# A graph network on one core: two of 208 groups of gathered rows are fetched row by row from two other queues

## The reference

```python
def reference(x, src, dst, edge_weight, edge_weight_n2, ...):       # x: 6250 x 256 f32, 106250 edges, dst sorted
    edge_index = jnp.stack([src, dst])
    x = _layernorm(x + _L0_gnn_ref(x, src, dst, edge_weight, edge_weight_n2, ...))
    x = _layernorm(x + _L1_gnn_ref(x, edge_weight, weight, bias, edge_index, 2))
    return x

def _L1_gnn_ref(feature, edge_weight, weight, bias, edge_index, mode):     # mode 2
    feature = feature - jnp.mean(feature, axis=0, keepdims=True)
    feature = feature / (jnp.std(feature, axis=0, ddof=1) + 0.0001)
    # _spmm: row edge_index[0] of the result is the sum over its edges of edge_weight * feature[edge_index[1]]
    support = _spmm(edge_index, edge_weight, feature, feature.shape[0])
    return support @ weight + bias
```

## Time and profile before

| | |
|---|---|
| median of 3 runs | 3402.89 us (3399.97 to 3411.76) |
| the profiled execution: its own time | 3413.44 us |
| the profiled execution: span of the profile | 3411.7 us |
| busy share of PE, PEld, DVE, ACT, POOL | 73%, 54%, 67%, 31%, 74% |
| DMA packets | 275056, 565.29 MB, mean 166 GB/s |

### The profile page before, as it was taken

One profiled execution on the slowest core, in us unless ns is written; L12 is line 12 of the kernel. 1 busy time (PEld: TensorE's weight loads), 2 busy tenths in 40 slices (PEclk: granted clock), 3 DMA queues, 4 the chain that ended last, 5 costly groups with the idle time before them and its releaser, 6 DMA issues.

```text
span 3411.7 us, 47557 instructions
## 1 busy us (share of the span) xinstructions
PE 2507.6 (73%) x10659; PEld 1840.3 (54%) x10701; DVE 2299.3 (67%) x5450; ACT 1059.9 (31%) x3135; POOL 2529.2 (74%) x2706
## 2 busy tenths in 40 slices
PE   5776766666676666579999999996776665556777
PEld 4555544444344443368888888543444444444565
DVE  7989977777777677657776777786455455555455
ACT  3344333333333333245555555562000000000022
POOL 6777677777777777777777777576777777777775
PEclk8878988888988889799999999998988888887899
DMA  6554344444444444388988999454333333333344
GB/s 163 157 147 126 120 158 154 158 162 155 157 155 156 163 155 156 129 262 285 289 288 284 291 290 292 153 172 136 105 105 105 105 105 105 105 105 106 109 137 120
DMA packets 275056, 565.29 MB, mean 166 GB/s; under 512 B 55599, under 2 KB 121126, under 8 KB 274787
## 3 DMA queue, kind: packets, MB, share of 16 engines
q0 software_dynamic: 119808, 329.02, 30.8%
q1 hardware_dynamic: 146452, 223.99, 20.8%
q10 hardware_dynamic: 8528, 9.30, 0.9%
HBM read 419.19 MB, written 142.88 MB: 165 GB/s over the span
## 4 chain that ended last, share of the span: by engine, by line
POOL 49%; PE 22%; issue 18%; DVE 7%; DMA 2%; ACT 1%; DVEq 1%; SPq 0%; POOLq 0%; ACTq 0%
POOL arena L630 23%; POOL messages L560 21%; PE ps L1152 11%; PE ps L962 8%; POOL arena L554 5%; PE ps L1185 2%; PE ps L1085 1%; DMA messages<-arena 1%; DVE ps L2037 1%; DVE ps L2036 1%; DMA arena<-messages 1%; ACT arena L739 0%; DVE bn L2018 0%; DVE ps L1605 0%; DVE ps L1606 0%
## 5 line engine op out<-in xcount | busy, mean ns | idle before, releaser
L560 POOL DMA_INDIRECT messages<-arena x832 | 803.8, 966 | 264.1 <-issue 249.0
L554 POOL DMA_INDIRECT arena<-in_x,arena x832 | 792.1, 952 | 272.3 <-issue 250.7
L630 POOL DMA_INDIRECT arena<-x_table,wh x832 | 790.0, 950 | 263.2 <-issue 253.4
L1222 PE MATMUL ps<-arena 128*128 x2048 | 603.0, 450 | 367.0 <-SPq L505 366.7
L1222 PEld LDWEIGHTS ps<-arena 128*128 128x128 f32 x2048 | 439.4, 223 | 536.6 <-issue 469.8
L962 PE MATMUL ps<-arena 128*128 128x128 f32 x3328 | 457.8, 296 | 127.6 <-ACT arena L676 89.9
L739 ACT ACTIVATE arena<-ps,arena 128x256 f32<-128x256 f32 x832 | 326.5, 475 | 703.3 <-PE ps L1085 466.0
L962 PEld LDWEIGHTS ps<-arena 128*128 128x128 f32 x3328 | 436.8, 209 | 193.1 <-ACT arena L676 128.9
L1085 PE MATMUL ps<-arena 128*128 128x256 f32 x1664 | 470.7, 434 | 49.6 <-DVE arena L1789 42.2
L2212 DVE TENSOR_TENSOR node_a<-node_a,ps 128x256 f32 x256 | 107.7, 421 | 503.7 <-PE ps L1222 501.6
L1085 PEld LDWEIGHTS ps<-arena 128*128 128x128 f32 x1664 | 364.2, 221 | 78.9 <-issue 23.9
(11 more groups left out here) (287 smaller groups left out, 2981.9 us busy)
## 6 DMA issues: line engine op xcount, KB each, us to landing
arena<-messages SPq DMA_DIRECT2D x464, 260.0 KB
arena<-in_x SPq DMA_DIRECT2D x304, 128.0 KB, 2.8
gate_rows<-arena SPq DMA_DIRECT2D x49, 384.0 KB, 2.4
arena<-gate_rows SPq DMA_DIRECT2D x49, 384.0 KB, 3.0
arena<-in_x,arena POOLq DMA_INDIRECT x832
messages<-arena POOLq DMA_INDIRECT x832, 2.5
arena<-x_table,wh POOLq DMA_INDIRECT x832, 2.8
arena<-in_x SPq DMA_DIRECT2D x48, 256.0 KB, 2.9
```

What stands on the lines that cost most here:

```text
L554: nc.gpsimd.indirect_dma_start(out=big[:, s, j, 0:D], out_offset=None, in_=x, in_offset=bass.IndirectOffsetOnAxis(ap=ids[:, j:j + 1], axis ...
L560: nc.gpsimd.indirect_dma_start(out=messages, out_offset=bass.IndirectOffsetOnAxis(ap=ids[:, j:j + 1], axis=0), in_=big[:, s, j, :], in_off ...
L630: nc.gpsimd.indirect_dma_start(out=last_rows[:, (g + 1) % LAST_ROWS, j * D:(j + 1) * D], out_offset=None, in_=x1_table, in_offset=bass.Ind ...
L1222: last = nc.tensor.matmul(ps[g % LAST_SUMS][:, 0:D], last_hot[h][:, j, :], last_rows[:, bass.ds(k, 1), j * D:(j + 1) * D].rearrange("p o d ...
```

## The change

Groups 170 and 180 (`LATE`) are no longer gathered by GpSimd. Their 2 x 512 rows are fetched one row to a DMA, each from the row number of a register: group 170 by ScalarE's queue, in one piece after the square root of line 852 and before the first finished tile; group 180 by SyncE's, four rows in each of the turns 12 to 139 of its loop over the groups. The two groups have buffers of their own, the ninth and tenth. To have the row numbers on one partition, SyncE stores the two groups' columns of `back_id` to memory in the gates stage and loads them back as one row of 1024 numbers. `slot_row` now holds the buffer in its upper bits, with eight more small operations on VectorE. TensorE takes count and buffer out of it, and shifts before it waits. The semaphores `xs_loaded` are named `rows_loaded` and used for both.

```diff
+LATE = (170, 180)
+ROWS_BITS = 8
...
+        BUFFERS = LAST_ROWS + len(LATE)
+        last_rows = arena[:, BACK_W:BACK_W + BUFFERS * CPG * D].rearrange("p (k c) -> p k c", k=BUFFERS)
...
+        def late_rows(engine, i, first, last):
+            for r in range(first, last):
+                p, j = r // CPG, r % CPG
+                v = engine.value_load(late_row[0:1, i * GE + r:i * GE + r + 1]).with_bounds(min_val=0, max_val=NT * P - 1)
+                engine.dma_start(last_rows[p:p + 1, LAST_ROWS + i, j * D:(j + 1) * D],
+                                 x1_table[bass.ds(v, 1), :]).then_inc(S[f"rows_loaded{i}"], 16)
...
             for t in range(3 * SPAN):
                 gates_load(t, t % GATES)
+            sp.wait_ge(S["back_kept"], 2 * PAIRS)
+            sp.wait_ge(S["back_mm"], 2 * PAIRS)
+            for i, g in enumerate(LATE):
+                sp.dma_start(late_table[i, :, :], back_id[:, g * CPG:(g + 1) * CPG]).then_inc(S["row_kept"], 16)
...
             gates_load(FULL, 0)
+            sp.wait_ge(S["row_kept"], 16 + 16 * len(LATE))
+            sp.dma_start(late_row, late_table.rearrange("(o i) p j -> o (i p j)", o=1)).then_inc(S["row_back"], 16)
...
+            sp.wait_ge(S["row_back"], 32)
+            sp.wait_ge(S["x1_stored"], 16 * (SPANS + 1))
             for g in range(GATHERED):
-                sp.wait_ge(S[f"second_rows{g % LAST_ROWS}"], (g // LAST_ROWS + 1) * 16 * CPG)
+                if g in LATE:
+                    sp.wait_ge(S[f"rows_loaded{LATE.index(g)}"], 16 * (2 * XPAIRS // RING + GE))
+                else:
+                    sp.wait_ge(S[f"second_rows{g % LAST_ROWS}"], rounds_of(g) * 16 * CPG)
                 sp.sem_inc(S["second_landed"], 1)
...
+                if 12 <= g < 12 + -(-GE // 4):
+                    late_rows(nc.sync, 1, (g - 12) * 4, min((g - 12 + 1) * 4, GE))
...
             for g in range(GATHERED):
                 k = g % LAST_ROWS
+                if g in LATE:
+                    continue
                 if g >= LAST_ROWS:
                     pool.wait_ge(S["second_freed"], g - LAST_ROWS + 1)
...
+            act.wait_ge(S["row_back"], 32)
+            act.wait_ge(S["x1_stored"], 16 * (SPANS + 1))
+            late_rows(nc.scalar, 0, 0, GE)
             ready = 0
             for g in range(FIRST_END, LAST + 1):
...
-                    rows = nc.tensor.value_load(slot_row[0:1, g:g + 1], min_val=1, max_val=GATHERED)
-                    k = (rows & (LAST_ROWS - 1)).with_bounds(min_val=0, max_val=LAST_ROWS - 1)
+                    slots = nc.tensor.value_load(slot_row[0:1, g:g + 1], min_val=1, max_val=GATHERED + (BUFFERS - 1 << ROWS_BITS))
+                    rows = (slots & ((1 << ROWS_BITS) - 1)).with_bounds(min_val=1, max_val=GATHERED)
+                    k = (slots >> ROWS_BITS).with_bounds(min_val=0, max_val=BUFFERS - 1)
...
+            link(V.tensor_scalar(buffer_i.bitcast(I32), slot_row, LAST_ROWS - 1, ROWS_BITS, ALU.bitwise_and, ALU.logical_shift_left))
+            link(V.tensor_copy(buffer_n, buffer_i.bitcast(I32)))
+            for i, g in enumerate(LATE):
+                moved = LAST_ROWS + i - (g + 1) % LAST_ROWS << ROWS_BITS
+                link(V.tensor_scalar(buffer_i, parts_n, float(g + 1), float(moved), ALU.is_equal, ALU.mult))
+                link(V.tensor_tensor(buffer_n, buffer_n, buffer_i, ALU.add))
+            link(V.tensor_tensor(parts_n, parts_n, buffer_n, ALU.add))
+            link(V.tensor_copy(slot_row, parts_n))
```

More of the change, by code:

```diff
@@ L107, in gnn_program @@
         weight_row = dram("weight_row", [NT * P])
+        late_table = dram("late_table", [len(LATE), P, CPG], I32)
         node_a = sb("node_a", [P, NTP, D])
@@ L234, in gnn_program @@
         last_hot = [hot[:, k, :, :] for k in range(2)] + [area(hot_at + 2304 + k * GE, [CPG, P]) for k in range(LAST_HOTS - 2)]
-        last_rows = arena[:, BACK_W:BACK_W + LAST_ROWS * CPG * D].rearrange("p (k c) -> p k c", k=LAST_ROWS)
-        assert LAST_ROWS & LAST_ROWS - 1 == 0 and BACK_W <= 4 * D + NC and BACK_W + LAST_ROWS * CPG * D <= COLUMNS_W + 2048
+        BUFFERS = LAST_ROWS + len(LATE)
+        last_rows = arena[:, BACK_W:BACK_W + BUFFERS * CPG * D].rearrange("p (k c) -> p k c", k=BUFFERS)
+        assert LAST_ROWS & LAST_ROWS - 1 == 0 and BACK_W <= 4 * D + NC and BACK_W + BUFFERS * CPG * D <= COLUMNS_W + hot_at
         assert PARTS % (4 * RING) == 0 and PARTS <= NG
+        late_row = area(hot_at + 3840, [len(LATE) * GE], I32)[0:1, :]
         slot_row = low_tab[0:1, 0:PARTS]
+        buffer_i, buffer_n = (area(hot_at + 4928 + k * PARTS, [PARTS])[0:1, :] for k in range(2, 4))
         parts_i, parts_n = (area(hot_at + 4928 + k * PARTS, [PARTS])[0:1, :] for k in range(2))
@@ L330, in units_of, with rounds_of @@
                     (v >> UNIT_BITS).with_bounds(min_val=0, max_val=NU - NT)]
+        def rounds_of(g):
+            return sum(1 for k in range(g % LAST_ROWS, g + 1, LAST_ROWS) if k not in LATE)
+        def late_rows(engine, i, first, last):
[4 more added lines that the diff above has]
+                                 x1_table[bass.ds(v, 1), :]).then_inc(S[f"rows_loaded{i}"], 16)
         def scales_of(g):
@@ L377, in x_load @@
                 sp.dma_start(xs[:, s, :].rearrange("p (t d) -> p t d", t=2),
-                             x[2 * q * P:(2 * q + 2) * P, :].rearrange("(t p) d -> p t d", p=P)).then_inc(S[f"xs_loaded{s}"], 16)
+                             x[2 * q * P:(2 * q + 2) * P, :].rearrange("(t p) d -> p t d", p=P)).then_inc(S[f"rows_loaded{s}"], 16)
             sp.dma_start(xt[0:TAIL, :], x[FULL * P:N, :]).then_inc(S["xt_loaded"], 16)
@@ L972, in x_sum @@
             def x_sum(i, s):
-                pe.wait_ge(S[f"xs_loaded{s}"], 16 * i)
+                pe.wait_ge(S[f"rows_loaded{s}"], 16 * i)
                 nc.tensor.matmul(ps[0][:, :], ones[:, :], xs[:, s, :], start=isinstance(i, int) and i == 1 and s == 0, stop=False).then_inc(S["x_used"], 1)
@@ L1479, in run @@
                 def run():
-                    dve.wait_ge(S[f"xs_loaded{s}"], 16 * (i - X_SHIFT + XPAIRS // RING + 1))
+                    dve.wait_ge(S[f"rows_loaded{s}"], 16 * (i - X_SHIFT + XPAIRS // RING + 1))
                     mean = ps[0][:, 0:D].rearrange("p (o d) -> p o d", o=1).broadcast_to([P, 2, D])
```

## The result

| | before | with the change |
|---|---|---|
| median | 3401.56 us (3399.97 to 3411.76, 4 runs) | 3439.99 us (3436.74 to 3441.84, 4 runs) |
| profiled execution: own time, span | 3413.44 us, 3411.7 us | 3436.74 us, 3434.6 us |

The ratio is 1.0106, with a 95% interval of 1.0093 to 1.0118: slower by 32 to 40 us. Forecast were 3392.8 us, in a range of 3388 to 3405, and a chance of 0.11 for slower.

What follows compares the result with a forecast made beforehand. GpSimd's 832 gathers, 1.254 us each, were taken to bound the last product. Eight fewer save 10.0 us, plus 0.05 us from a TensorE register operation: 3402.9 - 10.1 = 3392.8 us, range 3388 to 3405.

Steps and rivals of the forecast that it cites:

- What one takes: ScalarE's price of a fetched row: load 0.279, arithmetic 0.070, DMA 0.378, gaps 0.17 us, about 0.90 us.
- ScalarE's 512 rows: Group 170's fetch after line 852: 518 us available, 1.01 us a row; 461 us needed, landed 57 us early, no cost.
- Bounds of a row's price: Row fetches on both queues: from 0.63 us up to 1.07 us on SyncE and 0.97 on ScalarE, all said to fit.
- Rival A: The two queues delay each other's row DMAs, group 170 lands 43 us late, GpSimd waits 24 us: 3417 us, chance 0.09.
- Rival B: Register loads take 0.6 us, ScalarE's row 1.22 us, GpSimd waits 88 us: 3481 us, chance 0.02.
- SyncE's turn: SyncE's loop over groups: a turn with four rows takes 3.8 us and fits in a group's 5.02 us.
- the price of a gather: GpSimd in the last product: 1.254 us each, so eight gathers fewer save 10.0 us.
- TensorE caught up: TensorE in the last product: group 171's work comes 5.02 us early, absorbed after five or six groups, no cost at the end.
- rival C: GpSimd's gathers get slower beside the 1024 small DMAs, 5.8 us at worst: 3398.6 us, chance 0.13.
- GpSimd hardly waits for buffers: GpSimd's gathers in the last product before the change: concluded from minimum and median lying 4 ns apart.
- The tail's clock: Last part and product behind it: shifted by 10 us, the clock may give 0.8 us or take 2.9; counted 0.
- Small things: VectorE's eight operations and SyncE's index stores fall into waits; uncovered 3 and about 1.3 us; TensorE's register operation gives perhaps 0.05.

Runs made afterwards that it cites:

- act_alone: The changed kernel with only group 170 fetched row by row, by ScalarE; GpSimd gathers group 180 again: 3445.03 us, one run.
- act_spread: The changed kernel with ScalarE's rows begun earlier, 100 before its first squaring and 8 after each pair of squarings: 3397.64 us, ratio 0.9976 to the kernel before.
- batched: The changed kernel with four register loads first, then their four DMAs, on both queues: 3396.22 us, ratio 0.9975 to the kernel before.
- sp_alone: The changed kernel with only group 180 fetched row by row, by SyncE; GpSimd gathers group 170 again: 3403.67 us, ratio 0.9994 to the kernel before.
- later_group: The changed kernel with ScalarE fetching group 190 in place of 170, its rows issued as before: 3415.46 us, one run.
- three_groups: The changed kernel with groups 170, 104 and 196 off GpSimd, loads and DMAs in batches: 3388.81 us, ratio 0.9963 to the kernel before.

## Why the prediction was wrong

**The term that failed** is "What one takes" under *ScalarE's 512 rows*: 0.90 us. Measured are 0.477 us for the load, 0.037 for the arithmetic, 0.457 for the DMA and some 0.15 between them, 1.13 us a row. 0.20 us of the error are the load, 0.08 the DMA; arithmetic and gaps were 0.03 and 0.02 shorter than summed. The limit was 1.01 us. My nearest rows came from a load behind a DMA of 128 partitions, 0.262 us, and from ScalarE's loads beside its activations, and my upper bound treated only the DMA as uncertain. *Bounds of a row's price* should have had the load in it too.

The price of the load stood in the trace of the kernel before. SyncE writes one row of weights to memory there in one DMA (line 434, from one partition), and the next load behind it takes 0.454 us though it comes 17 us later; the first turn of its loop over the groups, whose last DMA was a store of three tiles (line 500), shows 0.452 us at 2369.6 us, where the median of the loop is 0.267:

```profile
L434 SPq DMA_DIRECT2D weight_row<-node_c x1: 304/304/304, 1437.9 to 1437.9; - x1
...
L328 SPq TENSOR_LOAD <-pair_row x1: 454/454/454, 1455.7 to 1455.7; - x1
...
L508 SPq TENSOR_LOAD <-tile_tabs x3: 266/267/452, 2369.6 to 2379.6; - x3
```

With 0.45 us for the load the sum would have been an estimated 1.07 us a row, past the limit. Both were single loads that a median hides. That they are dear for the reason that the rows' loads are is argued from the like times, not shown.

**Rival A had the place right and the price nearly, the cause wrong.** It gave 302 rows at 1.23 us and the rest at 0.90 us, the group 43 us late, a gap of 24 us and 3417 us, 23 us short of the time measured. The last row was issued at 3251.7 us, SyncE waited 60.3 us, GpSimd 43.6. The step from lateness to gap (some 19 us of slack, up to group 174) gives 60.3 - 19 = 41 us, and 43.3 were measured. But no queue held up the other: act_alone has the same loads and DMAs, and in the changed kernel ScalarE's row stays at 1.12 us in the median after SyncE's last one (3046 us). Rival B had the right instruction and too high a figure: 0.6 us, where 0.477 were measured; the floor of 600 ns in the Trainium skill (DMA: Bandwidth & Descriptors, Latency and other measured facts) does not hold here (0.279 us in the stages before), but as a warning on the load it was worth more than the chance of 0.02.

**SyncE's turn** was sized at 3.8 us. From line 533 to the end of the fourth DMA it takes 4.46 us in the median of the turns from 2450 to 3000 us in the changed kernel, and 4.98 at the longest. One of the long ones starts at 2601.8 us and the next turn at 2606.8 (lines 533, 536 and 346):

```profile
L533 SPq EVENT_SEMAPHORE  x2: 17/17/17, 2601.8 to 2606.8; - x2
...
L536 SPq TENSOR_LOAD <-tile_tabs x2: 425/432/438, 2601.9 to 2606.9; - x2
...
L346 SPq DMA_DIRECT2D arena<-x_table x4: 254/255/258, 2603.4 to 2606.4; - x4
```

Its own load of line 536 costs 0.43 instead of 0.267 us, being the first behind a one-row DMA, and the last of its four DMAs starts at 2606.4. This turn fills 4.9 of 5.0 us. The forecast margin of 1.2 us was 0.5 in the median and next to nothing in such a turn; that it held was partly luck, since the load was mis-sized here as on ScalarE.

**Right:** the price of a gather, 1.254 us and 10.0 us for eight (act_spread, batched: 8 and 9 us, the intervals take in 10). TensorE caught up even after the gap: from 3253 to 3300 us it is busy 46.0 of 47 us at a clock of 0.96, and the time behind the last gather is again 21.4 us. GpSimd's gathers did not get slower beside the small DMAs (rival C); line 662 from 2400 to 3200 us in the changed kernel:

```profile
L662 POOL DMA_INDIRECT arena<-x_table,wh x641 | 606.2, 946 | 195.4 <-issue 195.4
```

That GpSimd hardly waits for buffers in the kernel before was right too, but does not follow from minimum and median of its gathers: a duration holds no waiting. Its waits from 2350 us on show it, none being for a buffer:

```profile
POOL arena L630 <- issue: 253.4, 831, 0.3
```

**The tail's clock** was counted as 0, with 0.8 us to gain and 2.9 to lose. The changed kernel has the same tail as before, 21.4 us, with a granted clock of 0.82 in the 9 us from 4 us behind the last gather's start. In sp_alone, batched and later_group the clock of these 9 us was 1.00 and the tail 19.8 to 19.9 us; in act_spread and three_groups it was 0.81 and the tail 21.3 to 21.4. So the term moves the end by some 1.6 us, twice what the prediction had given for the gain, and nothing in the change's loss comes from it.

**Small things:** in the changed kernel the gates stage, from its first product to the first gather, took 199.3 us, before 198.1; 199.2 to 199.3 also in act_spread and batched and 199.1 in sp_alone and act_alone, but 198.4 in three_groups, which has the same added instructions and more. What that microsecond is stays open. It would explain part of what the gains lack.

## What to carry to other kernels

Before work is moved to a queue, price each instruction in the order in which it will stand there; a load behind another kind of DMA is another instruction. Look for that order in the whole trace and at single instructions, as a median hides the few that matter. A term with a limit needs its bounds on every part of it: 12% more than the limit cost four times the gain. And what an idle engine takes on must be finished before its own next work, whatever group it belongs to; if it can, let it begin early and batch its loads and its DMAs.

## What the runs showed that I had not expected

- A register load directly behind a DMA of one row took 0.47 to 0.50 us instead of 0.27 to 0.28, on both queues; behind a DMA of 16 pieces it did not, and behind those of 128 partitions not in the median (in stage 2, 0.272 us for 202 loads of line 397, but up to 0.86 us; many of the dear ones are the first of a pass of the loop, and why is open). Even 1.4 us later it still took 0.44 us (batched), and in the kernel before 0.45 us after 17 us.
- ScalarE's one-row DMA took 0.457 us behind a register load and 0.225 us behind another DMA; SyncE's 0.255 and 0.225. Why ScalarE's is so much dearer behind a load is open.
- Batches of four brought a row on ScalarE from 1.13 to 0.82 us.
